# Ranks of four radix sorts on Trainium2: the one-hot rows made lane by lane with a scalar comparison, and the rank picked out by one accumulating operation per lane

## What is computed

```python
att = (q[dst] * key_e).sum(-1) * rel_pri[etype] / sqrt_dk        # typed attention, sums by dst and type
ex = jnp.exp(att - m[seg]); den = jax.ops.segment_sum(ex, seg, num_segments=s)
...
msg = jax.ops.segment_sum(h[src], dst, num_segments=n_nodes)     # gated graph, six times
...
agg = jax.ops.segment_sum(msg, dst, num_segments=M)              # the router's graph attention
```

## Time and profile before

| | |
|---|---|
| median of 3 runs | 9392.7 us (9391.0 to 9400.03) |
| the profiled execution | 9396.04 us, span 9394.3 us |
| PE matmul busy | 6449.5 us (69%) |
| DVE busy | 3760.5 us (40%), 9083 instructions |
| POOL busy | 3364.2 us (36%) |
| ACT busy | 1459.4 us (16%) |

### The profile page before, as it was taken

The page is one execution under the profiler, slowest core; times in us unless marked ns, Lnnn a source line. Parts: engine busy times, 40 slices in busy tenths (PEclk is TensorE's granted clock), DMA queues, the critical chain, the costliest instruction groups (busy, mean ns, idle before and its releaser), DMA issues. The chain is left out here.

```text
span 9394.3 us, 97132 instructions
## 1 busy us (share of the span) xinstructions
PE 6449.5 (69%) x25098; PEld 4084.6 (43%) x25099; DVE 3760.5 (40%) x9083; ACT 1459.4 (16%) x2467; POOL 3364.2 (36%) x4319
## 2 busy tenths in 40 slices
PE   5548454384677266729736479999999999755556
PEld 3323232142343133328612245666666565544445
DVE  7871596011565766521189611111111111233522
ACT  0001000010111000002135022222222222111001
POOL 0457755677565177237510057000000000067022
PEclk9999555697666566759979589999999999855568
DMA  2002000121233023126500221111111111000035
GB/s 86 3 16 72 11 0 2 41 74 45 70 91 74 23 86 87 41 73 195 157 11 1 89 70 46 49 42 49 42 53 46 46 53 46 27 8 7 1 93 181
DMA packets 417206, 518.27 MB, mean 55 GB/s; under 512 B 171883, under 2 KB 338280, under 8 KB 417000
## 3 DMA queue, kind: packets, MB, share of 16 engines
q1 hardware_dynamic: 300392, 375.92, 12.5%
q0 software_dynamic: 116608, 139.65, 5.9%
HBM read 388.58 MB, written 126.19 MB: 55 GB/s over the span
## 5 line engine op out<-in xcount | busy, mean ns | idle before, releaser
L863 POOL COPY gs_from_ids<-gat_src_row 128x8 uint16 (+1 forms) x80 | 16.2, 202 | 2363.9 <-SPq L115 2363.6
L2161 PE MATMUL gg_p_all<-gg_edges,gg_other 128*128 128x384 f32 (+3 forms) x2700 | 808.9, 458 | 3.3 <-DVE gg_other L2322 3.3
L2161 PE MATMUL gg_p_all<-gg_edges,nodes 128*128 128x384 f32 (+3 forms) x2700 | 808.5, 458 | 2.8 <-DVE nodes L2322 2.8
L2161 PEld LDWEIGHTS gg_p_all<-gg_edges,gg_other 128*128 128x128 f32 (+1 forms) x2700 | 497.4, 190 | 304.0 <-issue 30.7
L2161 PEld LDWEIGHTS gg_p_all<-gg_edges,nodes 128*128 128x128 f32 (+1 forms) x2700 | 497.5, 190 | 302.4 <-issue 30.8
L2334 DVE SCALAR_TENSOR_TENSOR gg_move<-gg_p_all,gg_b_state,gg_gates 128x384 f32<-128x384 f32 (+2 forms) x108 | 62.2, 576 | 1314.6 <-PE gg_p_all L2184 1314.6
L1250 PE MATMUL ha_p_sum<-ha_weighted,ha_hot 128*128 128x257 f32 x832 | 388.0, 629 | 257.4 <-DVE sums L1214 246.3
L354 POOL DMA_INDIRECT cell_sorted<-cell_scatter_what,cell_scatter_at x400 | 429.9, 1075 | 174.4 <-issue 94.9
L354 POOL DMA_INDIRECT hgt_once<-hgt_scatter_what,hgt_scatter_at x400 | 413.0, 1032 | 174.5 <-issue 94.1
L868 POOL DMA_INDIRECT ha_values<-v_table,ha_value_rows x416 | 406.8, 978 | 182.7 <-issue 92.2
L2005 PE MATMUL ce_p_cell<-ce_hot_at,ce_hot_src 128*128 128x512 f16 (+1 forms) x1280 | 256.0, 327 | 302.2 <-DVE ce_hot_src L1965 156.1
(11 more groups left out here) (485 smaller groups left out, 11518.0 us busy)
## 6 DMA issues: line engine op xcount, KB each, us to landing
gg_packed<-cell_counts SPq DMA_DIRECT2D x150, 800.0 KB, 4.3
e_w<-in_L_ffn_W_dram SPq DMA_DIRECT2D x64, 1024.0 KB
e_w<-in_L_ffn_W_dram SPq DMA_DIRECT2D x56, 512.0 KB
k_table<-hp_kr SPq DMA_DIRECT2D x25, 1024.0 KB, 4.6
v_table<-hp_kr SPq DMA_DIRECT2D x25, 1024.0 KB, 7.4
cell_counts<-cell_acc SPq DMA_DIRECT2D x5, 4000.0 KB
slots<-clear_zeros SPq DMA_DIRECT2D x15, 1024.0 KB, 13.4
e_rows<-slots SPq DMA_DIRECT2D x60, 256.0 KB, 4.9
```

The source lines that it names most:

```text
L2161: mm = pe.matmul(p_all[:, half, 0:n], rows[0:some, t, half * P:(half + 1) * P], edges[0:some, turn % 2, t, 0:n], start=t == 0, stop=t == t ...
```

## The change

In both loops `hot` is made by four operations in place of one: per lane a `tensor_scalar` that compares a constant row of column numbers (bf16) with one value per partition, the digit of that lane's column. For that `digit` becomes float32. In the rank loop the product, the wait behind it and the sum go; in their place stand four `scalar_tensor_tensor`, one per lane, which compare the column numbers with the digit again, multiply by the lane's `rank` in PSUM, write `prod`, and put the sum of the row straight into `place` (`accum_out`). The counts that TensorE waits for are multiplied by four, so it still starts when all four lanes of a step are there. The semaphore `reduced` goes.

```diff
-    digit = sb("digit", [P, chunks], BF16)
+    digit = sb("digit", [P, chunks])
...
-    by_lane = digit[:, :].rearrange("p (q j) -> p q j", q=lanes)
-    place_lane = place[:, :].rearrange("p (q j) -> p q j", q=lanes)
-    count = g.count_bf[:, 0:digits].unsqueeze(1).to_broadcast([P, lanes, digits])
+    count = g.count_bf[:, 0:digits]
...
         def one_hot(j, b):
-            dve.tensor_tensor(hot[:, b, :, :], by_lane[:, :, bass.ds(j, 1)].to_broadcast([P, lanes, digits]),
-                              count, ALU.is_equal).then_inc(hot_ready, 1)
+            for q in range(lanes):
+                dve.tensor_scalar(hot[:, b, q, :], count, digit[:, bass.ds(j + q * runs, 1)], None,
+                                  ALU.is_equal).then_inc(hot_ready, 1)
...
-                dve.tensor_tensor(prod[:, b, :, :], rank[:, :, 0:digits], hot[:, b, :, :],
-                                  ALU.mult).then_inc(prod_ready, 1)
-                gate(dve, g, prod_ready, j + 1)
-                dve.tensor_reduce(place_lane[:, :, bass.ds(j, 1)], prod[:, b, :, :].unsqueeze(2), AX,
-                                  ALU.add).then_inc(reduced, 1)
+                for q in range(lanes):
+                    at = bass.ds(j + q * runs, 1)
+                    dve.scalar_tensor_tensor(out=prod[:, b, q, :], in0=count, scalar=digit[:, at],
+                                             in1=rank[:, q, 0:digits], op0=ALU.is_equal, op1=ALU.mult,
+                                             accum_out=place[:, at]).then_inc(prod_ready, 1)
...
-                pe.wait_ge(hot_ready, i * 2 + (b + 1 + runs))
+                pe.wait_ge(hot_ready, i * (2 * lanes) + (b + 1 + runs) * lanes)
...
-                pe.wait_ge(prod_ready, i * 2 + (b + 1))
+                pe.wait_ge(prod_ready, i * (2 * lanes) + (b + 1) * lanes)
```

More of the change, by code:

```diff
@@ L208, in rank_words @@
     rank_moved = g.sem(f"{tag}_rank_moved")
-    reduced = g.sem(f"{tag}_reduced")
     filled = g.sem(f"{tag}_filled")
     padded = g.sem(f"{tag}_padded")
-    by_lane = digit[:, :].rearrange("p (q j) -> p q j", q=lanes)
-    place_lane = place[:, :].rearrange("p (q j) -> p q j", q=lanes)
-    count = g.count_bf[:, 0:digits].unsqueeze(1).to_broadcast([P, lanes, digits])
+    count = g.count_bf[:, 0:digits]
     block = g.block
@@ L280, in rank_body @@
                 dve.wait_ge(rank_ready, j + 1)
-                dve.tensor_tensor(prod[:, b, :, :], rank[:, :, 0:digits], hot[:, b, :, :],
-                                  ALU.mult).then_inc(prod_ready, 1)
-                gate(dve, g, prod_ready, j + 1)
-                dve.tensor_reduce(place_lane[:, :, bass.ds(j, 1)], prod[:, b, :, :].unsqueeze(2), AX,
-                                  ALU.add).then_inc(reduced, 1)
+                for q in range(lanes):
[3 more added lines that the diff above has]
+                                             accum_out=place[:, at]).then_inc(prod_ready, 1)
         one_hot(0, 0)
         peeled(dve, runs // 2, rank_body)
-        dve.wait_ge(reduced, runs)
+        dve.wait_ge(prod_ready, lanes * runs)
         ch.step(dve.tensor_copy(t0[:, :], place[:, :]))
@@ L302, in hist_body @@
             for b in range(2):
-                pe.wait_ge(hot_ready, i * 2 + (b + 1))
+                pe.wait_ge(hot_ready, i * (2 * lanes) + (b + 1) * lanes)
                 for q in range(lanes):
```

## The result

The changed kernel takes 9556.3 us (median of 4 runs, 9548.3 to 9561.7) against 9393.6 for the kernel before on the same chip: ratio 1.0171, 95% interval [1.0154, 1.0189], slower. The profiled execution took 9559.4 us, its span 9557.7.

The account below looks back on a forecast made before the run. VectorE's rank and histogram work was taken to bound phases A, B, D and F, with four of five ranks exposed. Rank loops +333 and histogram loops +16 on 9396.0 gave 9745 us, 9742 on the median's scale; range 9570 to 9960.

Parts of the forecast that it names:

- the term A: Rank loop: cost of putting out the row sum per accumulating operation, taken as 0.10 us, between 0 and 0.23.
- the clock: TensorE's clock might drop in phases A and B; four matmuls at 128 digits would still take 0.61 us.
- Rival 1: Rank loop: the row sum comes free with the accumulating operation; +201 us, 9594; chance 0.20.
- The chain: Rank loop: comparisons must wait for TensorE's four from matmuls, which the removed sum had covered; 2.12 becomes 3.05 us at 128 digits.
- the formula: Rank step: matmul time plus 0.20 us of handover, four comparisons and four accumulating operations; rank loops +333 us.
- T: Time of one lane-wise comparison in both loops: 0.17, 0.21 and 0.157 us for 128, 201 and 51 digits.
- Half the rate for lanes 1 and 3: Comparisons at 201 and 51 digits: these lanes begin mid-word and run at half rate, giving 0.21 and 0.157 us.
- Rival 3: Comparisons miss the fast rate, one column per 1.04 ns; 143 us more in rank, 72 in histogram loops, 9957; chance 0.05.
- Histogram loops: Two steps 1.57 us against 1.50 at 128 digits, 1.97 against 2.04 at 201, 1.26 against 0.91 at 51; together +16.
- the register operations run ahead of VectorE while it is busy: Both loops: one register operation per small instruction, costed at nothing.
- Phase E: Rank of gat pass 0 grows by about 86 us but stays hidden behind POOL; VectorE idle before G some 80 us.
- Rival 4: Phase E: each comparison of gat pass 0 stops POOL's scatters; +91 us, 9833; chance 0.05.

Follow-up runs that it names:

- e1_compare_only: Kernel before with only the one-hot made by four lane-wise comparisons, product and sum as before; 9407.4 us, 1.0009 against the kernel before.
- e2_accum_only: Kernel before with only product and sum replaced by four accumulating operations, one-hot as before; 9534.1 us, 1.0144 against the kernel before.
- e4_sum_back: Changed kernel with its four operations writing only the product and the removed sum put back behind them; 9565.5 us, 1.0174 against the kernel before.
- e7_before_four_buffers: Kernel before with four one-hot buffers in place of two and loops unrolled by four; 9383.4 us, 0.9904 against the kernel before.
- e10_turns_for_hgt: Lane-by-lane turns of comparison and accumulating operation for both hgt passes, the kernel before with four one-hot buffers for the rest; 9197.0 us, 0.9789.
- e8_two_in_turn: Changed kernel, four one-hot buffers in the histogram loop, comparison and accumulating operation taking turns lane by lane in the rank loop; 9449.2 us, 0.9977.

## Why the prediction was wrong in size and right in kind

- **The step that failed** is the term A, "what putting out the row sum costs", taken as 0.10 us from the row of a tiny operation that nobody waits for. It measures 0.01: 0.27 us between accumulating operations, 0.26 between the same ones without a sum. From A = 0.10 to A = 0 the forecast falls from 9742 to 9594, which is 148 of the 186 us that it missed by. The range took that case in and stopped 24 us below it, while other terms were off by 38 us together: 25 in stretches without an exposed rank, 18 in D, less some in A, B and F. In D two things that the forecast did not have, the faster comparisons and the clock (below), made the loss smaller.
- The Trainium skill, "VectorE: DVE Perf Modes", § Two Vector instructions with no wait between them, was used against A = 0. The trace agrees that there are two instructions, the second 0.08 us long. It does not follow that they cost time one after the other: the read starts when the next operation starts. Rival 1, A = 0, given 0.20, is what happened; its 9594 is 38 us above the result.
- **The chain** was right. At A = 0 the formula gives 2.65, 3.36 and 2.02 us a step; the means of the loops are 2.63, 3.27 and 2.00. The idle time before the first comparison, 0.82, 1.06 and 0.57, was forecast as 0.81, 1.05 and 0.55. That the removed sum was worth nothing because it had stood in that time is shown by putting it back.
- **T** was 0.17, 0.21 and 0.157. Four comparisons take 0.66, 0.75 and 0.58 us to the next operation's start in the means of the rank loops, so T measured 0.164, 0.19 and 0.144. Half the rate for lanes 1 and 3 was assumed at 201 and 51 digits and is not there: at 201 digits the comparisons of all lanes start 0.18 us apart (medians). With 0.75 for the four the formula gives the measured 3.27. This is 8 us of D. Rival 3 is out.
- **Histogram loops**: +16 forecast, +20 measured, and not where it was said. Two steps at 128 digits 1.65 instead of 1.57; at 51 digits 1.44 instead of 1.26, since 0.20 us of issue time per iteration shows once eight short operations have no wait that covers it: "the register operations run ahead of VectorE while it is busy" failed there. At 201 digits it went the other way. The granted clock rose in the middle of the loop, which the forecast had considered only in the other direction. Windows of the trace before, then two of the trace after:

```profile
1033.00:1085.00 52.00, 42.47 (x200) 21.52 (x200) 49.07 (x51) 0.00 (x0) 41.63 (x37) 0.50 0.01 0
```

```profile
1148.00:1200.00 52.00, 43.44 (x213) 22.97 (x214) 44.53 (x216) 0.00 (x0) 37.10 (x53) 0.50 0.02 1
1200.00:1239.00 39.00, 25.35 (x188) 13.98 (x188) 37.07 (x185) 0.00 (x0) 27.87 (x39) 0.98 0.02 1
```

  TensorE's matmuls fell from 0.86 to 0.53 us for four, VectorE's comparisons ran on with no wait, and the loop took 91 us, where it had taken 103 before and 3.5 less was forecast. D so grew by 11 us, where the formula with A = 0 gives 33 - 3.5: 8 us of the difference are in this loop and 8 in the rank loop (T, above).
- **Phase E** cost nothing, as said, and VectorE's idle time before G is 98 us; 80 was forecast with A = 0.10.
- **Rival 4**, POOL held up, went the other way. In the histogram loop of D, beside comparisons back to back, a scatter takes 0.97 us, where beside the old one-hot it took 1.73:

```profile
1200.99 2.77 DVE L232 TENSOR_SCALAR hgt_rank_hot<-count_bf,hgt_rank_digit 128x201 bf16<-128x201 bf16 x13 [0.34 <-PE hgt_rank_hist L303]
1201.49 0.98 POOL L352 DMA_INDIRECT cell_sorted<-cell_scatter_what,cell_scatter_at  x1 [0.30 <-issue]
```

  The halves say the same for the whole loop: the median scatter takes 0.97 us in `e1_compare_only` (comparisons by lane) and 1.73 in `e2_accum_only` (the old one-hot). E got shorter by 6 us and POOL's busy time in the whole program by 68 us (3364 to 3296). Of the 6 us some 4 go with the comparisons: E takes 308.0 to 309.1 us in every kernel that has them there, and 312.5 to 314.5 in every one that has the old one-hot. The Trainium skill's rule in "SBUF — State Buffer", § SBUF: two separate sides, by which the fast comparison would shut POOL out, shows in this row at most as 0.01 us. But each comparison here moves the next by only 0.18 us, so whether a long one would hold POOL up is not shown. What stretched the scatters was the `tensor_tensor` with two SBUF inputs. Its length alone does not explain it, since the 39 scatters that ran mostly beside the equally long sum (0.99 us, one input) stay at 0.97 to 0.99 in the trace before.

## What to carry to other kernels

When an operation is removed between two engines that take turns, ask first what it was covering: here the sum and the gap ahead of it hid a round of 0.8 us through TensorE, and their removal only uncovered the wait. The leaner set of operations paid here only with an order in which each wait is for something that was started a good part of a step earlier; hand-over in parts (by lane or by pair) gave that in the rank loop with two buffers. Together with four buffers in the histogram loop and the old operations at 64 and 51 digits it turned +1.7% into -2.5%, on chips where the kernel before takes 9394 us. Where operations have a fixed part (about 0.14 us each here), four in place of one pay for long rows and lose for short ones, so choose the form by the size.

## What the hardware showed that was not expected

- An accumulated row sum on VectorE costs 0.01 us per operation, though its read is a record of 0.08 us. It is so at all three sizes (0.267, 0.344 and 0.188 us from start to start with it, 0.258, 0.334 and 0.178 without).
- `tensor_scalar` comparisons of 16-bit rows leave POOL's indirect DMA issues at 0.97 us; the `tensor_tensor` one-hot stretched them to 1.73.
- The granted clock of TensorE rose from 0.50 to 0.98 in the histogram loop of phase D (1.2 to 2.4 GHz) after TensorE had been busy there for 43.4 of 52 us. In the kernel before it was busy for 42.5 of 52 us in the same loop and stayed at 0.50. It rose there in `e1_compare_only` and `e4_sum_back` too, and not in `e2_accum_only`, which has the old one-hot. In `e7_before_four_buffers`, the old one-hot with four buffers, it went up and down. What lifts it is not shown.
- On two chips, where the kernel before takes 9472 us instead of 9394, loops of many small operations with hand-overs had steps of up to three times the length and more while POOL scattered, and exact ones from its last scatter on. On three others such loops ran evenly beside the same scatters. The loops of before, with one large operation for four small ones, ran evenly on either sort at 126 and 201 digits (their rank step with four buffers was 2.09 to 2.10 us in nearly all of B on a chip where the kernel before takes 9472 us). At 64 digits, where that operation too takes only 0.34 us, they did not: the histogram loop of E took 43 us in `e7_before_four_buffers` against 24 in `e10_turns_for_hgt`, which has the same loop there. The cause stays open, and so does whether pairs of lanes would resist it. On such a chip the fastest kernel here may lose much of its gain: `e8_two_in_turn`, its near relative, had 0.9977 there, the kernel before with four buffers 0.9904.
